# A GRU and mixture-of-experts kernel: the hidden bias of the candidate gate moves from VectorE's reset operation to a TensorE matmul

## The chip, the cores and the metric

The kernel runs on one core of one Trainium2 chip. The metric is the device time of one execution in microseconds; the time before is 849.63 us, the median of 3 runs (849.52 to 850.55). TensorE multiplies, and writes its results to PSUM; VectorE, ScalarE and GpSimd (POOL in the profile) do the elementwise work; SyncE (SP) and ScalarE issue the loads and stores.

## The reference, cut to what matters

The first half is a GRU over 4 sequences of 512 steps with a state of 512, the second a mixture of four experts on its output. Only the GRU's cell is touched:

```
def cell(h, x):
    gi = x @ W_ih + b_ih
    gh = h @ W_hh + b_hh
    i_r, i_z, i_n = jnp.split(gi, 3, axis=-1)
    h_r, h_z, h_n = jnp.split(gh, 3, axis=-1)
    r = sigmoid(i_r + h_r)
    z = sigmoid(i_z + h_z)
    n = tanh(i_n + r * h_n)
    return (1.0 - z) * n + z * h
```

The last third of `b_hh`, here called b_hn, is inside `h_n` and so is multiplied by r. It can't be folded into the input part, as the other two thirds are. After the GRU come the logits `h @ Wg + bg`, the top two of four experts for each token, a capacity of 512 tokens per expert, and per expert gelu(tok @ W1) @ W2, scaled and added into the output.

## The kernel before, in words

**The steps.** Each sequence is cut into 16 segments that run side by side, so that a step works on 64 columns (4 sequences by 16 segments, COLS). A segment has 32 steps; before them each segment runs 40 steps over the input ahead of it to find its starting state: 20 rough ones (ROUGH) that use only the high fp16 half of weights and state, and then 20 exact ones. So there are 72 steps: 20 rough ones and 52 exact ones. Numbers are split into a high and a low fp16 half, and an exact product is three products (high by high, high by low, low by high).

**A step on the engines.** The state has four blocks of 128 rows (j = 0 to 3). The gates of block j lie in PSUM bank j, 64 columns each for r, z and the candidate. TensorE first adds the input part of r and z into the bank by a matmul with a diagonal matrix (`inject`, line 452), which waits until the `reset` of block j of the step before is done (semaphore rn_done, line 450). The matmul that carries start=True clears the bank's marks, so the candidate's 64 columns are overwritten by the first matmul that comes to them. Then come the matmuls with the weights (`unit`, line 442, 64 columns each, three for a product of blocks): 12 for each block k of the state in a rough step, in the order k = 0 to 3; 144 in an exact step, in the order written out as ORDER (line 261). Each k waits for the new state's block k (high_ready, line 490).

When bank j is done, ScalarE takes the sigmoid of r and z (`sig`, line 758), VectorE does `reset` (line 1203: candidate part plus b_hn times r) and `candidate_in` (line 1208: plus the input part), ScalarE the tanh (line 763), VectorE `one_less_z` (line 1212) and `blend` (line 1219, the state's high half, which releases TensorE), and in exact steps `keep_state` (line 1224). GpSimd makes z times h (`carry`, line 931) and the low halves of blocks 0 and 1 (line 939), VectorE those of blocks 2 and 3. The order on VectorE is written out by hand (`exact` and `rough`, lines 1245 to 1252):

```
exact = ((reset, 0), (candidate_in, 0), (reset, 1), (candidate_in, 1), (reset, 2),
         (one_less_z, 0), (candidate_in, 2), (blend, 0), (keep_state, 0), (one_less_z, 1),
         (reset, 3), (blend, 1), (candidate_in, 3), (one_less_z, 2), (keep_state, 1), (blend, 2), ...
```

ORDER begins with the injects of banks 0 and 1, the unit of bank 1 with block 0 of the state, the inject of bank 2, the units of banks 0 and 2 with block 0, the inject of bank 3, and then a unit with block 1.

**The fills.** The products of the input with W_ih (`fill`, line 434, 512 columns) are made ahead: the first chunk in fp32 before the steps (lines 407 and 417), 24 matmuls just before the first step, and then 18 in each of the steps 0 to 21 and 12 in step 22. In rough steps they are spread over k by FILLS = (13, 2, 2, 1). Between its step work VectorE also splits these products and the recurrent weights (`other_work`).

**Before the steps.** VectorE takes the absolute maxima of all that is loaded (line 1062), from them the scales (lines 1090 to 1099 and 1139 to 1143), then splits W_ih (line 1118) and the first chunk of x (line 1124, `x_low`), whose semaphore x_split releases the first fill. ScalarE's queue issues two loads of W_ih and five small loads, of which that of bg (line 688) is the last.

Of the kernel before, what the change touches and what calls it, by code (L numbers as in the profile page):

```python
# [14 lines left out]
ALU = mybir.AluOpType  # L15
ACT = mybir.ActivationFunctionType
AX = mybir.AxisListType
RMAX = bass.bass_isa.ReduceOp.max
F32 = mybir.dt.float32
F16 = mybir.dt.float16  # L20
# [3 lines left out]
P = 128  # L24
# [9 lines left out]
SEARCH_PASSES = 10  # L34


def gru_moe(nc, x, x_t, cond_t, w_ih, w_hh, b_ih, b_hh, wg, bg, w1, w2, hs_rows, out):
    NB, T, D = x.shape
    N = NB * T
    E, _, H = w1.shape  # L40
# [15 lines left out]
    with ExitStack() as ctx:  # L56
        def sb(name, shape, dt=F32):
            return ctx.enter_context(nc.sbuf_tensor(name, shape, dt))
# [54 lines left out]
        def gru_tmp(n):  # L113
# [62 lines left out]
        un_y = sb("un_y", [P, 1])  # L176
        un_gates = sb("un_gates", [P, 1])
        gates_scale = sb("gates_scale", [P, 1])
        bhn_s = sb("bhn_s", [P, KD])
        neg_scale = sb("neg_scale", [P, 1])  # L180
        worst = sb("worst", [P, 4])
        flag = sb("flag", [P, SEG + 1], I32)
# [41 lines left out]
        names = """small_loaded out_init consts_pool consts_dve bias_ready  # L224
             gi_mm gi_high gi_low gi_kept diag_ready sig_done gates_known gi_known x_known wih_high wih_split whh_high x_high x_split peak_ready peak_known chain whh_ready zh_done warmed high_ready state_done low_ready last_low_ready gates_mm rn_done
            candin_ready tanh_done ocand_done start_saved check_a worst_ready worst_mm flag_ready
            gru_over turned wg_split lg_mm lg_kept sq_done probs_in probs_stored group_made rows_copied rows_stored steps_made exp_in exp_done
            above_ready chunk_peaks total_mm masks_ready sums_ready eq_mm sel_ready pos_mm pos_ready slots_ready list_mm idx_ready
            tok_turned tokT_ready ffn1_mm hid_ready ffn2_mm y_ready scattered latched w_peak w_peak_all w_scaled w_high w_low prep hid_made hid_high y_scaled tok_high
            tables again orders_made first_high first_low root rechain sp_waited pool_waited dve_waited pe_waited act_waited pool_consts""".split()  # L230
# [165 lines left out]
        def _(pe):  # L396
# [51 lines left out]
            def inject(j, c, cols, parts, steps):  # L448

                pe.wait_ge(S["rn_done"], steps + j + 1)  # L450
                for part in parts:
                    pe.matmul(gate_ps[:, j, 0:2, :], diag[:, :], gi_rz[:, c, j, part, :, cols],  # L452
                              start=(part == HIGH), stop=False, skip_group_check=True)

            def logits(i):

# [40 lines left out]

            fill(0, PREFILL)
            pe.wait_ge(S["diag_ready"], 1)
            pe.wait_ge(S["whh_high"], KD)  # L500
            pe.wait_ge(S["gi_kept"], 12)
            for i in range(ROUGH):
# [177 lines left out]
        def _(act):  # L680
# [7 lines left out]
            act.dma_start(bg_sb[:, :], bg.rearrange("(o e) -> o e", o=1).to_broadcast([P, E])).then_inc(S["small_loaded"], 16)  # L688

            act.wait_ge(S["consts_dve"], 1)  # L690
            act.activation(worst[:, 3:4], ones[:, 0:1], ACT.Sigmoid).then_inc(S["tables"], 1)
            act.wait_ge(S["tables"], 1)

# [327 lines left out]

        @block.vector
        def _(dve):
            dve.memset(ones[:, :], 1.0).then_inc(S["consts_dve"], 1)
            dve.memset(onesb[:, :], 1.0)
            dve.memset(flag[:, :], 0)
# [32 lines left out]
            def peak_of(dst, src, axes=AX.XY):  # L1059

                link_n[0] += 1
                dve.tensor_reduce(dst, src, axes, ALU.max, apply_absolute_value=True).then_inc(S["chain"], 1)

            for k in range(2):
                dve.wait_ge(S["first_loaded"][k], 32)
                peak_of(x_peak[:, k:k + 1], x_first[:, 2 * k:2 * k + 2, :])
                peak_of(chunk_peak[:, k:k + 1], wih_sb[:, 2 * k:2 * k + 2, 0:D])
            dve.wait_ge(S["wih_loaded"][1], 16)
            peak_of(chunk_peak[:, 2:3], wih_sb[:, :, D:2 * D])
            dve.wait_ge(S["small_loaded"], 16 * 5)  # L1070
# [38 lines left out]
            def rz_low(t):  # L1109

                c, m = TILES[t]
                dve.wait_ge(S["gi_high"], rz_count(t + 1))
                dve.tensor_tensor(gi_rz[:, c, m % 4, LOW, m // 4, :], gi_full[:, rz_count(t) % GI_RING, :],
                                  gi_rz[:, c, m % 4, HIGH, m // 4, :], ALU.subtract).then_inc(S["gi_low"], 1)
# [24 lines left out]
            dve.tensor_tensor(un_gates[:, :], unscale[:, WHH:WHH + 1], unscale[:, STATE:STATE + 1], ALU.mult)  # L1139
            link(dve.tensor_tensor(gates_scale[:, :], scale[:, WHH:WHH + 1], scale[:, STATE:STATE + 1], ALU.mult))  # L1140
            dve.tensor_scalar(neg_scale[:, :], scale[:, STATE:STATE + 1], -1.0, None, ALU.mult)
            dve.tensor_scalar(bhn_s[:, :], bhh[:, 8:12], gates_scale[:, 0:1], None, ALU.mult)
            link(dve.tensor_scalar(bsum_g[:, :], bsum[:, :], gates_scale[:, 0:1], None, ALU.mult))
            dve.sem_inc(S["gates_known"], 1)
            wih_low(0)
# [15 lines left out]
            for m in range(ACT_HIGHS, 8):  # L1161
                rz_high(m)
                rz_low(m)

            def whh_low(n):

# [22 lines left out]
            def step(gi_n, after, src, base, low, moved=False, ahead=(), between=()):  # L1189
# [10 lines left out]

                def reset(j):
                    dve.wait_ge(S["sig_done"], base + j + 1)
                    dve.scalar_tensor_tensor(rn[:, j, :], gate_ps[:, j, 2, :], bhn_s[:, j:j + 1], rz[:, j, 0, :],  # L1203
                                             ALU.add, ALU.mult).then_inc(S["rn_done"], 1)

                def candidate_in(j):
                    dve.wait_ge(S["rn_done"], base + (KD + j + 1))
# [446 lines left out]
def laid_out(inputs):  # L1654

    x = np.asarray(inputs['x'])
    nb, t, d = x.shape
    kd, steps = d // P, t // SEG

    x_t = x.reshape(nb * SEG, steps, kd, P).transpose(3, 2, 1, 0).reshape(P, kd, -1, 512).transpose(0, 2, 1, 3)  # L1660
    return {
        'x': x,
        'x_t': x_t,
        'cond_t': np.asarray(inputs['cond_2048']).reshape(nb, kd, P).transpose(2, 1, 0),
        'w_ih': inputs['L0_cond_W_ih'],
        'w_hh': inputs['L0_cond_W_hh'],
        'b_ih': np.asarray(inputs['L0_cond_b_ih']).reshape(-1, P).T,
        'b_hh': np.asarray(inputs['L0_cond_b_hh']).reshape(-1, P).T,
        'wg': np.asarray(inputs['L0_ffn_Wg']).reshape(kd, P, -1).transpose(1, 0, 2),
        'bg': inputs['L0_ffn_bg'],  # L1670
        'w1': inputs['L0_ffn_W1'],
        'w2': inputs['L0_ffn_W2'],
    }
# [19 lines left out]
```

## Time and profile before

| | |
|---|---|
| median of 3 runs | 849.63 us |
| the profiled execution | 849.56 us, of which the span from first to last instruction is 847.8 us |
| TensorE (PE) busy | 806.1 us, 95% of the span |
| VectorE (DVE) busy | 621.8 us, 73% |
| ScalarE (ACT) busy | 422.8 us, 50% |
| GpSimd (POOL) busy | 184.7 us, 22% |
| chain that ended last | PE 83%, DVE 11%, issue 2%, ACT 2%, DMA 1% |
| the steps | from 58.45 us to about 446 us of the span |

A matmul's busy time in the profile is its latency (193 ns for 64 columns), and many of them overlap; how closely they follow each other is read from the starts of the rows of a timeline, or from the chain of waits, whose pieces lie end to end.

### The profile page before, as it was taken

How to read it: one execution, taken by the hardware profiler on the slowest of the kernel's cores; microseconds unless marked ns; L12 is line 12 of the kernel's file. 1: busy time of each engine (PE TensorE's matmuls, PEld its weight loads, DVE VectorE, ACT ScalarE, POOL GpSimd, SP SyncE). 2: the span in 40 equal slices, each digit the busy share in tenths (PEclk: the TensorE clock that was granted, in tenths of full speed). 3: DMA queues.
4: the chain of work that ended last, by engine and by line, in shares of the span. 5: the costliest groups of instructions: out<-in, count | busy, mean ns of one | idle time of the engine just before them, and what ended most of it. 6: DMA issues, size and time to landing. Idle time of an engine off the chain costs nothing.

```text
span 847.8 us, 27827 instructions
## 1 busy us (share of the span) xinstructions
PE 806.1 (95%) x11579; PEld 520.9 (61%) x11580; DVE 621.8 (73%) x2104; ACT 422.8 (50%) x884; POOL 184.7 (22%) x459
## 2 busy tenths in 40 slices
PE   7999999999999999999995789999999999999996
PEld 3446656588989899999983444444444444544442
DVE  6969899868888888888886988685768566855400
ACT  0677676645566555555553437451745175417500
POOL 1002222223433333343330030121012101210011
PEclk9999999999999999999996999999999999999998
DMA  9900000000111010000002942454245424540011
GB/s 334 358 3 3 2 2 2 2 3 16 54 54 42 17 41 5 4 4 4 5 4 52 246 155 95 155 148 101 88 160 150 98 84 164 141 107 0 1 26 25
DMA packets 24280, 62.61 MB, mean 74 GB/s; under 512 B 4384, under 2 KB 4384, under 8 KB 22304
## 3 DMA queue, kind: packets, MB, share of 16 engines
q1 hardware_dynamic: 19312, 51.42, 18.0%
q0 software_dynamic: 3584, 8.42, 5.4%
q8 instruction: 86, 1.41, 0.7%
q10 hardware_dynamic: 1264, 1.08, 0.4%
q14 instruction: 34, 0.28, 0.1%
HBM read 52.49 MB, written 12.62 MB: 77 GB/s over the span
## 4 chain that ended last, share of the span: by engine, by line
PE 83%; DVE 11%; issue 2%; ACT 2%; DMA 1%; POOLq 0%; DVEq 0%
PE ps L442 22%; PE ps L649 20%; PE ps L662 20%; PE ps L434 10%; PE ps L417 3%; DVE wa L1203 3%; DVE wa L1208 2%; PE ps L452 2%; PE ps L407 2%; DVE halves L1219 2%; ACT wa L758 2%; PE ps L636 1%; DMA hx<-hs_rows,idx 1%; DVE ocand L1212 1%; PE ps L590 1%
## 5 line engine op out<-in xcount | busy, mean ns | idle before, releaser
L442 PE MATMUL ps<-halves,wa 128*128 128x64 f16 x8448 | 287.6, 193 | 5.6 <-DVE halves L1219 1.8
L442 PEld LDWEIGHTS ps<-halves,wa 128*128 128x128 f16 x8448 | 271.0, 98 | 33.1 <-DVE halves L1219 14.1
L662 PE MATMUL ps<-big 128*128 128x512 f16 x768 | 166.9, 379 | 0.0
L649 PE MATMUL ps<-hx,big 128*128 128x512 f16 x768 | 166.9, 379 | 0.0
L758 ACT ACTIVATE wa<-ps,un_gates 128x128 f32<-128x128 f32 x288 | 100.2, 366 | 106.6 <-PE ps L442 100.2
L662 PEld LDWEIGHTS ps<-big 128*128 128x128 f16 x768 | 75.2, 98 | 89.9
L649 PEld LDWEIGHTS ps<-hx,big 128*128 128x128 f16 x768 | 74.9, 98 | 89.9 <-issue 0.2
L763 ACT ACTIVATE wa<-wa,un_gates 128x64 f32<-128x64 f32 x288 | 99.1, 344 | 59.8 <-DVE wa L1208 53.3
L1203 DVE SCALAR_TENSOR_TENSOR wa<-ps,bhn_s,wa 128x64 f32<-128x64 f32 x288 | 80.0, 278 | 52.9 <-ACT wa L758 52.9
L434 PE MATMUL ps<-hx,wb 128*128 128x512 f16 x432 | 106.9, 379 | 1.0 <-issue 1.0
L840 ACT ACTIVATE hx<-ps,un_hid_in 128x512 f32<-128x512 f32 x64 | 43.7, 682 | 109.2 <-PE ps L649 109.2
L1219 DVE SCALAR_TENSOR_TENSOR halves<-ocand,neg_scale,wa 128x64 f16<-128x64 f32 (+1 forms) x288 | 86.2, 299 | 4.6 <-DVE ocand L1212 0.5
L1464 DVE SCALAR_TENSOR_TENSOR big<-wa,scale,big 128x2048 f16<-128x2048 f32 x28 | 65.3, 2349 | 25.0 <-ACT big L826 25.0
L1582 DVE SCALAR_TENSOR_TENSOR big<-hx,hid_scale,big 128x512 f16<-128x512 f32 x64 | 47.8, 749 | 36.2 <-ACT big L843 35.1
L826 ACT ACTIVATE big<-wa,scale 128x2048 f16<-128x2048 f32 x28 | 54.8, 1988 | 34.1 <-DVEq L1452 34.1
L1208 DVE TENSOR_TENSOR wa<-wa,big 128x64 f32<-128x64 f32 x288 | 65.8, 228 | 5.0
L452 PE MATMUL ps<-big,diag 128*128 128x128 f16 x496 | 62.1, 219 | 0.8 <-DVE wa L1203 0.4
L1212 DVE SCALAR_TENSOR_TENSOR ocand<-wa 128x64 f32<-128x64 f32 x288 | 62.4, 217 | 0.2
L1410 DVE TENSOR_REDUCE chunk_peak<-wa 128x1 f32<-128x2048 f32 x28 | 62.0, 2277 | 0.0
L434 PEld LDWEIGHTS ps<-hx,wb 128*128 128x128 f16 x432 | 37.9, 98 | 35.7 <-issue 1.8
L931 POOL TENSOR_TENSOR wa<-wa,hx 128x64 f32<-128x64 f32 x128 | 42.6, 333 | 78.9 <-ACT wa L758 74.3
L997 POOL DMA_INDIRECT out<-hx,idx_out x16 | 29.0, 1815 | 136.1 <-DVE hx L1588 136.1
(209 smaller groups left out, 711.8 us busy)
## 6 DMA issues: line engine op xcount, KB each, us to landing
wa<-in_w SPq DMA_DIRECT2D x28, 1024.0 KB, 5.3
hs_rows<-big SPq DMA_DIRECT2D x8, 512.0 KB, 5.6
big<-in_w_hh SPq DMA_DIRECT2D x4, 768.0 KB, 19.4
wb<-in_w SPq DMA_DIRECT2D x12, 256.0 KB, 2.6
big<-in_w_ih SPq DMA_DIRECT2D x2, 1024.0 KB, 12.4
hx<-in_x_t SPq DMA_DIRECT2D x2, 1024.0 KB, 16.4
big<-in_w_ih ACTq DMA_DIRECT2D x2, 512.0 KB, 6.7
wa<-in_x_t SPq DMA_DIRECT2D x2, 512.0 KB, 6.3
```

Of the source, the lines that this page charges most:

```text
L434: mm = pe.matmul(ps[:, gi_bank(tile), :], wih_parts[:, w, k, m * P:(m + 1) * P], x_parts[:, q, t, k, :], start=(left == 0), stop=(left == ...
L442: mm = pe.matmul(gate_ps[:, j, g, :], whh_parts[:, k, w, (4 * g + j) * P:(4 * g + j + 1) * P], halves[:, src, k, h, :], start=False, stop= ...
L452: pe.matmul(gate_ps[:, j, 0:2, :], diag[:, :], gi_rz[:, c, j, part, :, cols], start=(part == HIGH), stop=False, skip_group_check=True)
L649: mm = pe.matmul(ps[:, m % 2, :], w1p[:, w, k, m * P:(m + 1) * P], tokT[:, t, k, :], start=(k == 0 and n == 0), stop=(k == KD - 1 and n == 2))
L662: mm = pe.matmul(ps[:, 2 + g % 2, :], hid[:, h, k, g * P:(g + 1) * P], w2p[:, w, k, :], start=(k == 0 and n == 0), stop=(k == KH - 1 and n ...
L758: act.activation(rz[:, j, :, :], gate_ps[:, j, 0:2, :], ACT.Sigmoid, scale=un_gates[:, 0:1]).then_inc(S["sig_done"], 1)
L763: act.activation(cand[:, j, :], cand_in[:, j, :], ACT.Tanh, scale=un_gates[:, 0:1]).then_inc(S["tanh_done"], 1)
L1203: dve.scalar_tensor_tensor(rn[:, j, :], gate_ps[:, j, 2, :], bhn_s[:, j:j + 1], rz[:, j, 0, :], ALU.add, ALU.mult).then_inc(S["rn_done"], 1)
L1208: dve.tensor_tensor(cand_in[:, j, :], rn[:, j, :], gi_n(j), ALU.add).then_inc(S["candin_ready"], 1)
L1212: dve.scalar_tensor_tensor(ocand[:, j, :], rz[:, j, 1, :], -1.0, cand[:, j, :], ALU.add, ALU.mult).then_inc(S["ocand_done"], 1)
L1219: dve.scalar_tensor_tensor(high_of(j), old(ocand_, j), neg_scale[:, 0:1], old(zh_, j), ALU.mult, ALU.add).then_inc(S["high_ready"], 1)
L1464: dve.scalar_tensor_tensor(w_parts[which][:, LOW, cols], stage[:, cols], scale[:, which:which + 1], w_parts[which][:, HIGH, cols], ALU.mul ...
```

## The change

b_hn is added by one more matmul in `inject`, with a stationary operand of 64 partitions. It is zero but for partition 0, which holds b_hn rounded to fp16 (scaled), and partition 32, which holds what the rounding left over. The moving operand is a 64 by 64 block of one value. `reset` becomes a product of two tensors. The row is loaded twice by ScalarE's queue, and VectorE makes the two halves in the part before the steps.

```diff
@@ inject
                 for part in parts:
                     pe.matmul(gate_ps[:, j, 0:2, :], diag[:, :], gi_rz[:, c, j, part, :, cols],
                               start=(part == HIGH), stop=False, skip_group_check=True)
+                pe.matmul(gate_ps[:, j, 2, :], bhn_parts[:, j * P:(j + 1) * P], bhn_unit[:, :], start=False, stop=False,
+                          skip_group_check=True)
@@ TensorE, before the first step
             pe.wait_ge(S["diag_ready"], 1)
+            pe.wait_ge(S["bhn_split"], 1)
@@ ScalarE, after its seven loads
             act.wait_ge(S["consts_dve"], 1)
+            for row in ROW_OF:
+                act.dma_start(bhn_row[row:row + 1, :], b_hn).then_inc(S["bhn_loaded"], 16)
             act.activation(worst[:, 3:4], ones[:, 0:1], ACT.Sigmoid).then_inc(S["tables"], 1)
@@ VectorE, its first instruction
+            dve.memset(bhn_row, 0.0)
             dve.memset(ones[:, :], 1.0).then_inc(S["consts_dve"], 1)
@@ VectorE, after the maxima of the first halves of x and of W_ih's first third
+            dve.wait_ge(S["bhn_loaded"], 32)
+            b_peak, b_scale, b_un = (bhn_scales[:, i:i + 1] for i in range(3))
+            link(dve.tensor_reduce(b_peak, bhn_row, AX.X, ALU.max, apply_absolute_value=True))
+            link(dve.tensor_scalar(b_peak, b_peak, 1e-30, None, ALU.max))
+            link(dve.tensor_scalar(b_un.bitcast(I32), b_peak.bitcast(I32), 0x7F800000, None, ALU.bitwise_and))
+            dve.tensor_scalar(b_scale.bitcast(I32), b_un.bitcast(I32), -1.0, float((254 + SCALE_TO) << 23),
+                              ALU.mult, ALU.add)
+            link(dve.tensor_scalar(b_un.bitcast(I32), b_un.bitcast(I32), -float(SCALE_TO << 23), None, ALU.add))
+            link(dve.tensor_scalar(bhn_parts[:, :], bhn_row, b_scale, None, ALU.mult))
+            lows_row = slice(ROW_OF[1], ROW_OF[1] + 1)
+            dve.scalar_tensor_tensor(bhn_parts[lows_row, :], bhn_row[lows_row, :], b_scale[lows_row, :],
+                                     bhn_parts[lows_row, :], ALU.mult, ALU.subtract)
             dve.wait_ge(S["wih_loaded"][1], 16)
             peak_of(chunk_peak[:, 2:3], wih_sb[:, :, D:2 * D])
@@ VectorE, at the scales of the gates
-            dve.tensor_scalar(bhn_s[:, :], bhh[:, 8:12], gates_scale[:, 0:1], None, ALU.mult)
@@ VectorE, before the first step
+            dve.tensor_scalar(bhn_unit[:, :], ones[0:COLS, 0:COLS], b_un, gates_scale[0:COLS, 0:1], ALU.mult,
+                              ALU.mult).then_inc(S["bhn_split"], 1)
@@ reset
-                    dve.scalar_tensor_tensor(rn[:, j, :], gate_ps[:, j, 2, :], bhn_s[:, j:j + 1], rz[:, j, 0, :],
-                                             ALU.add, ALU.mult).then_inc(S["rn_done"], 1)
+                    dve.tensor_tensor(rn[:, j, :], gate_ps[:, j, 2, :], rz[:, j, 0, :], ALU.mult).then_inc(S["rn_done"], 1)
```

`ROW_OF` is (0, 32); `bhn_row` is the first 64 partitions of the tile `carried` (512 fp32 values each), which the steps use later; `bhn_parts` is 64 by 512 in fp16, `bhn_unit` 64 by 64 in bf16. `link` makes VectorE wait for the instruction it has just issued.

## Rows read from the trace of the kernel before

**Rows 1.** Groups of instructions by line and shape: count, busy us, mean ns of one, idle before
```profile
L442 PE MATMUL ps<-halves,wa 128*128 128x64 f16 x8448 | 287.6, 193 | 5.6 <-DVE halves L1219 1.8
...
L1203 DVE SCALAR_TENSOR_TENSOR wa<-ps,bhn_s,wa 128x64 f32<-128x64 f32 x288 | 80.0, 278 | 52.9 <-ACT wa L758 52.9
...
L1208 DVE TENSOR_TENSOR wa<-wa,big 128x64 f32<-128x64 f32 x288 | 65.8, 228 | 5.0
...
L1224 DVE SCALAR_TENSOR_TENSOR hx<-ocand,neg_scale,wa 128x64 f32<-128x64 f32 x128 | 36.6, 286 | 0.0
```

**Rows 2.** Chain of waits, a rough step: start us, length us, what
```profile
133.44 2.81 PE ps L434 x13
...
136.30 0.09 PE ps L442 x3
...
138.95 2.81 PE ps L434 x13
```

**Rows 3.** Timeline, an exact step: start us, length of the merged group us, engine, line
```profile
344.48 1.16 ACT L758 ACTIVATE wa<-ps,un_gates 128x128 f32<-128x128 f32 x3 [1.61 <-PE ps L442]
...
345.53 0.73 ACT L763 ACTIVATE wa<-wa,un_gates 128x64 f32<-128x64 f32 x2
...
345.99 0.21 DVE L1212 SCALAR_TENSOR_TENSOR ocand<-wa 128x64 f32<-128x64 f32 x1
...
346.22 0.38 PE L452 MATMUL ps<-big,diag 128*128 128x128 f16 x4
346.31 0.28 DVE L1219 SCALAR_TENSOR_TENSOR halves<-ocand,neg_scale,wa 128x64 f16<-128x64 f32 x1
...
346.65 0.35 PE L442 MATMUL ps<-halves,wa 128*128 128x64 f16 x6
...
347.04 0.41 DVE L1219 SCALAR_TENSOR_TENSOR halves<-ocand,neg_scale,wa 128x64 f16<-128x64 f32 x1
347.06 0.30 POOL L939 TENSOR_TENSOR halves<-hx,halves 128x64 f16<-128x64 f32 x1
...
347.29 0.28 PE L452 MATMUL ps<-big,diag 128*128 128x128 f16 x2
...
347.50 0.46 PE L442 MATMUL ps<-halves,wa 128*128 128x64 f16 x10
...
349.57 0.37 ACT L758 ACTIVATE wa<-ps,un_gates 128x128 f32<-128x128 f32 x1 [1.60 <-PE ps L442]
```

**Rows 4.** Timeline of TensorE at rough step 11
```profile
121.82 2.97 PE L434 MATMUL ps<-hx,wb 128*128 128x512 f16 x13
125.02 0.23 PE L452 MATMUL ps<-big,diag 128*128 128x128 f16 x1 [0.23 <-DVE halves L1219]
```

**Rows 5.** Timeline of VectorE before the steps, with its idle time and what ended it
```profile
11.60 3.40 DVE L1062 TENSOR_REDUCE chunk_peak<-big 128x1 f32<-128x1024 f32 x2
15.50 0.17 DVE L1071 TENSOR_TENSOR bsum<-bih,bhh 128x8 f32<-128x8 f32 x1 [0.49 <-DMA bg_sb<-in_bg]
...
21.32 4.54 DVE L1062 TENSOR_REDUCE x_peak<-hx 128x1 f32<-128x2048 f32 x3 [0.21 <-DMA hx<-in_x_t]
...
48.96 1.41 DVE L1124 SCALAR_TENSOR_TENSOR hx<-hx,scale 128x512 f16<-128x512 f32 x2
```

**Rows 6.** Timeline of TensorE at the first fill
```profile
50.47 1.89 PE L434 MATMUL ps<-hx,wb 128*128 128x512 f16 x8 [1.02 <-issue]
```

**Rows 7.** Timeline of ScalarE's queue: the last of its small loads is issued
```profile
4.26 0.49 ACTq L688 DMA_DIRECT2D bg_sb<-in_bg  x1
```

**Rows 8.** DMA issues by line: count, KB each, median us from issue to landing
```profile
bhh<-in_b_hh ACTq DMA_DIRECT2D x1, 6.0 KB, 8.9
...
bg_sb<-in_bg ACTq DMA_DIRECT2D x1, 2.0 KB, 11.2
```

**Rows 9.** Stretches: length us, busy time per engine, granted clock share (PEclk), DMA share, GB/s
```profile
455.70:460.63 4.93, 4.91 (x35) 4.29 (x36) 2.85 (x14) 2.35 (x4) 0.00 (x0) 0.50 0.01 2
...
494.76:498.18 3.42, 3.42 (x11) 1.86 (x10) 1.38 (x2) 0.97 (x2) 0.81 (x1) 0.50 0.41 131
```

More of the change, by code:

```diff
@@ L34, with gru_moe @@
 SEARCH_PASSES = 10
-def gru_moe(nc, x, x_t, cond_t, w_ih, w_hh, b_ih, b_hh, wg, bg, w1, w2, hs_rows, out):
+def gru_moe(nc, x, x_t, cond_t, w_ih, w_hh, b_ih, b_hh, b_hn, wg, bg, w1, w2, hs_rows, out):
     NB, T, D = x.shape
@@ L178, in gru_moe @@
         gates_scale = sb("gates_scale", [P, 1])
-        bhn_s = sb("bhn_s", [P, KD])
+        bhn_row = carried[0:COLS, :, :, :].rearrange("p d k c -> p (d k c)")
+        bhn_parts = sb("bhn_parts", [COLS, D], F16)
+        bhn_unit = sb("bhn_unit", [COLS, COLS], BF16)
+        bhn_scales = sb("bhn_scales", [COLS, 4])
+        ROW_OF = (0, 32)
         neg_scale = sb("neg_scale", [P, 1])
@@ L226, in gru_moe @@
             candin_ready tanh_done ocand_done start_saved check_a worst_ready worst_mm flag_ready
-            gru_over turned wg_split lg_mm lg_kept sq_done probs_in probs_stored group_made rows_copied rows_stored steps_made exp_in exp_done
+            gru_over turned bhn_loaded bhn_split wg_split lg_mm lg_kept sq_done probs_in probs_stored group_made rows_copied rows_stored steps_made exp_in exp_done
             above_ready chunk_peaks total_mm masks_ready sums_ready eq_mm sel_ready pos_mm pos_ready slots_ready list_mm idx_ready
@@ L1668, in laid_out @@
         'b_hh': np.asarray(inputs['L0_cond_b_hh']).reshape(-1, P).T,
+        'b_hn': np.asarray(inputs['L0_cond_b_hh'])[2 * d:].reshape(1, -1),
         'wg': np.asarray(inputs['L0_ffn_Wg']).reshape(kd, P, -1).transpose(1, 0, 2),
```

## The prediction

> **What bounds the kernel now.** I read the chain of waits first, since TensorE's 95% is an average over parts with different limits. The chain shows two kinds of steps, and before them a part that ends on VectorE.
>
> Rough steps with fills belong to TensorE. In [rows 2] the pieces lie end to end and the step repeats after 138.95 - 133.44 = 5.51 us, with VectorE nowhere in it. Two paces come from here: 0.09 / 3 = 0.029 us for a matmul of 64 columns, 2.81 / 13 = 0.216 for one of 512. Steps 20 to 22 carry their fills at the head and are alike up to bank 0 of step 22, so 23 steps belong to TensorE.
>
> Exact steps without fills repeat after 349.57 - 344.48 = 5.09 us [rows 3], and here the timeline says more than the chain. The four injects start at 346.22 and, by 0.38 less their latency of about 0.22 over three gaps, follow each other by 0.055, so TensorE could go on at 346.44. It goes on at 346.65, 0.05 after blend 0 ended (346.31 + 0.28). Then it comes to block 1: the last injects start at 347.29 and 347.35, it could go on at 347.40, and it goes on at 347.50, 0.05 after blend 1 ended (347.04 + 0.41). So TensorE stands 0.21 and 0.10 us per step. From 347.50 it runs through 63 matmuls to the end of bank 0 and the next sigmoid. The loop is: sigmoid 0, three resets and candidates on VectorE, one_less_z 0, blend 0, blend 1, TensorE. It holds steps 22 to 70, 49 periods.
>
> Before the steps TensorE stands 1.02 us ahead of its first fill [rows 6]. The profile gives no releaser, but the last x_low ends at 48.96 + 1.41 = 50.37 and the fill starts at 50.47 [rows 5, 6]: VectorE's preparation ends last. It waits only briefly for loads after 11.60 (0.49, 0.21, and two alike of 0.30 and 0.21), and from 21.32 it works nearly without a gap [rows 5].
>
> **The change, part by part.** *The added matmuls.* Four per step, 288 in all. No matmul with 64 partitions is in the trace. The nearest row is the 64-column one [rows 1]: its pace of 0.029 us is my value. It could be as low as nothing where TensorE stands anyway, and as high as 0.33, if the array had to empty before and after it (latency 0.193 less 0.029, twice). In the 23 steps that belong to TensorE, nothing hides them: 23 x 4 x 0.029 = +2.7 us. In step 11 TensorE stands for VectorE: the fills from 121.82 end at 121.82 + 13 x 0.216 = 124.63 and the inject starts at 125.02 [rows 4], 0.39 us. Later arrival of TensorE and shorter resets close this: -0.4. Sum for these steps: +2.3.
>
> *The reset.* It becomes a product of two tensors. The other kind of instruction with a per-partition operand and both inputs in SBUF takes 286 ns, reset with an input in PSUM 278, the tensor product or sum without such an operand 228 [rows 1]. So the 50 to 60 ns hang on that operand and not on PSUM; I take 0.22, and a saving of 0.055 in length and in the distance to the next instruction. Its bounds are 0 and 0.065. In an exact step three resets lie ahead of blend 0, which would be 0.165. But one_less_z 0 needs tanh 0, and that one starts at 345.53 behind sigmoid 2 on ScalarE and ends at about 345.87, whatever VectorE does [rows 3]. one_less_z can start at 345.90 instead of 345.99: the saving is capped at 0.09. All behind it moves by 0.09, blend 1 included, which ends at 347.36, and TensorE may go on at 347.41.
>
> *The added matmuls in an exact step.* Two come before blend 0 and fit into the 0.21 that TensorE stands (0.12 left with the earlier blend). Two lie between blend 0 and the units of block 1: from 346.56, 18 x 0.029 + 4 x 0.055 + 2 x 0.029 = 0.81, so 347.37, still ahead of 347.41. They are hidden, by 0.04. If a reset saved nothing, they would still fit into the 0.10. So an exact step gains 0.09, and 49 of them -4.4 us (bounds 0 and, see below, -6.6).
>
> *VectorE before the steps.* The new block waits for two loads and stands ahead of the maxima of W_ih's second third, at 12.73, ahead of the second reduction in the group at 11.60 (whose end, 15.00, less the 2.27 of 2048 elements, is where it starts) [rows 5]. The loads are issued behind bg's, which is issued at 4.26 for 0.49 [rows 7], so at about 4.8 and 5.3. bg lands at 4.26 + 11.2 = 15.5, small ones need 8.9 or more [rows 8]: between 14.2 and 17, I take 16.0. Then come a maximum over 512 elements (2.27 for 2048 gives 1.1 ns each; 0.7 with its start and its link), three linked small ones at 0.2, one at 0.1, a scaling of 512 elements, 0.5, and a subtraction on one partition but 512 long, 0.7: 2.6 us. So the second third begins at 18.6 instead of 12.73. VectorE had 1.2 us of waits for loads behind this point, and these and no more take it up, with the bias sum now behind its load: it is at the scales 4.3 us later. From there to the last x_low nothing is idle that could give it back, and TensorE's first fill starts 4.3 us later. Queued behind VectorE's wait are the scales (ScalarE waits on them for its whole part before the steps) and x_low, for which TensorE waits. With the load at 14.2 it is 2.5, with 17 it is 5.3, and if the load were there when VectorE comes, 1.1. The memset of 512 elements at the start, about 0.5 us at that rate, lies beside VectorE's wait for the first loads; without that cover it would cost itself. The product for bhn_unit, 0.2 us, lies beside the 24 fills.
>
> *The clock.* TensorE then stands 5 us instead of 1. In two places of the trace TensorE comes back to dense work after it stood for some us, and both times it works at a granted clock of 0.50 first: through the 4.93 us before 460.63, and 3.42 us from 494.76 [rows 9]. At half clock half of such a stretch is lost: 1.7 us, bounds 0 and 2.5.
>
> **The sum.** +4.3 + 1.7 + 2.3 - 4.4 = +3.9. The profiled execution took 849.56, 847.8 of it the span and 1.8 around it; the median of the runs, 849.63, is the same within 0.1. So 847.8 + 3.9 + 1.8 = 853.5 us.
>
> **The rivals.** *The array empties at each added matmul.* It uses half the rows, between matmuls that use all. For it: nothing in the trace mixes the two. Against: nothing either. The price from the latency is 0.33 per added matmul. Rough and fill steps: 23 x 4 x 0.33 = 30. In an exact step the path from blend 0 gets 2 x 0.33 and the pair before it some 0.6 beyond its cover, so about 1.1 in place of a gain of 0.09: 55. With the part before the steps: near 940 us. The Trainium skill, "TensorEngine Tiling (Array Packing)", section "Key Properties", says that changing the tiling mode, not just the tile, drains TensorE, and lists a contraction of 64 or less as the case for row tiling; the trace of before can't show it. By that rule the sum would be the one of this rival, without it the one above. I give it 0.14.
>
> *The load is early (the other side).* If the row is in SBUF when VectorE comes to it, the block costs 2.6 less the waits behind it, 1.1, TensorE stands 2 us, and the clock stays: 1.1 + 2.3 - 4.4 = -1.0, so 848.6. It decides from a landing before about 14, where the time falls below that of before. For it: it is 2 KB to one partition, and bg's load, 128 rows, was the slowest of the five. Against: it is issued behind bg on the same queue, while the large loads run. 0.15.
>
> *The reset is no shorter from PSUM.* Then the exact steps gain nothing: 847.8 + 8.3 + 1.8 = 857.9. Against: PSUM is no dearer in reset's own row. 0.09.
>
> *Blend 1 loses its stretch.* It takes 0.41 where blend 0 takes 0.28, and GpSimd's low half starts 0.02 behind it [rows 3]. Moved ahead by 0.09 it may end before the two meet. Then TensorE's own path, 347.37, is last, and a step gains 0.135: -6.6 in place of -4.4, 851.3. 0.12.
>
> **How the numbers follow.** The forecast has 0.50. Its own range is 850.9 to 856.5, from the bounds of landing, clock and the cap. The range over the cases is 847.5 to 862: it holds the early load, the missing saving and a dearer matmul of up to 0.1 in rough steps, and leaves the emptying array out. Under 0.2% (1.7 us) this kernel's measurement can't tell from no change. Faster needs the early load together with the blend's gain or a still smaller block: 0.11. The same: most of the rest of the early load, and the low end of the blend case, 0.14. Slower 0.75.
>
> **What would show it.** Right: an added matmul 0.03 us behind the inject before it; rough steps of 5.63 us; reset at 0.22 us; exact steps of 5.00 us with TensorE standing less than 0.1 before blend 0's units; VectorE's wait for the row ending near 16 and the first fill near 54.8; a granted clock of half for about 3.4 us behind it. Wrong: exact steps of 5.09 or more, a first fill before 53, rough steps above 5.7 us, which would be the emptying array, or an idle time of VectorE ahead of the resets that takes the gain back.

## The result, and the profile after

The changed kernel takes 900.99 us (median of 4 runs, 899.23 to 901.1) beside 849.75 for the kernel before on the same chip: a ratio of 1.0596, with an interval of 1.0578 to 1.0615. The forecast was 853.5 us with a range of 847.5 to 862, so it is wrong, and by far. What happened is close to what the prediction named as its first rival: the added matmul costs TensorE far more than its 64 columns. The profiled execution has a span of 897.5 us, 49.7 more than before. It is the shortest of the four (899.23); the other three took 900.91 to 901.10, at a mean granted clock of 0.982 to 0.983 beside its 0.985.

The page's head and its busy times:

```profile
span 897.5 us, 28413 instructions
...
PE 859.3 (96%) x11867; PEld 547.7 (61%) x11868; DVE 616.6 (69%) x2112; ACT 421.0 (47%) x884; POOL 183.9 (20%) x459
```

The groups by line and shape (count, busy us, mean ns of one, idle before) that answer to [rows 1]:

```profile
L446 PE MATMUL ps<-halves,wa 128*128 128x64 f16 x8448 | 297.1, 193 | 0.9 <-DVE halves L1242 0.8
...
L1231 DVE TENSOR_TENSOR wa<-wa,big 128x64 f32<-128x64 f32 x288 | 71.7, 249 | 5.0
...
L1227 DVE TENSOR_TENSOR wa<-ps,wa 128x64 f32<-128x64 f32 x288 | 63.0, 219 | 107.6 <-ACT wa L767 107.6
...
L458 PE MATMUL ps<-bhn_unit,bhn_parts 64*128 64x64 bf16 x288 | 57.5, 200 | 0.0
```

The added matmul (L458) has a mean of 200 ns, only 7 more than a unit (L446). That mean hides its cost: a matmul's length here is mostly latency, and several are under way at once. What it costs is in the distances between starts. The reset (L1227) did become shorter, 219 ns for 278, yet VectorE's wait ahead of it doubled, from 52.9 us to 107.6: the gain was in an engine that now waits longer.

A rough step in the chain of waits (start us, length us, what; in the chain a piece lasts only until the next one takes over), as in [rows 2]:

```profile
142.99 2.81 PE ps L438 x13
145.80 0.06 PE ps L456
145.85 0.13 PE ps L458
145.99 0.19 PE ps L446 x3
```

Before, the inject (L452 there) took 0.06, in the same chain as [rows 2]:

```profile
136.25 0.06 PE ps L452
```

With the three units behind it that was 0.06 + 0.09 = 0.15 us. Now inject, added matmul and units take 0.06 + 0.13 + 0.19 = 0.38. The chain puts only 0.13 on the added matmul; the rest, 0.10, is on the three units behind it, which took 0.09 before. So a reader of the chain alone would find only half of the cost under the new line.

TensorE in an exact step (start us, length of the merged group us), answering to [rows 3]:

```profile
351.38 0.27 PE L456 MATMUL ps<-big,diag 128*128 128x128 f16 x2
351.59 0.20 PE L458 MATMUL ps<-bhn_unit,bhn_parts 64*128 64x64 bf16 x1
351.72 0.28 PE L456 MATMUL ps<-big,diag 128*128 128x128 f16 x2
351.94 0.20 PE L458 MATMUL ps<-bhn_unit,bhn_parts 64*128 64x64 bf16 x1
352.07 0.35 PE L446 MATMUL ps<-halves,wa 128*128 128x64 f16 x6
```

The second inject of the pair at 351.38 starts at about 351.43, and the added matmul only at 351.59; the next inject starts 0.13 behind it. Medians over all steps of the distance from start to start: inject to added 152 ns, added to unit 132, added to inject 132, where before inject to inject is 56 and unit to unit 29. So each added matmul costs about 0.10 us ahead of it, 0.10 behind it, and 0.03 of its own: 0.152 + 0.132 - 0.056 = 0.228 us. The state is ready all this time. TensorE no longer stops for VectorE at 352.07, where it stopped in [rows 3]: its own path is longer than VectorE's.

Where the 49.7 us are, from the start of the first inject of each step:

| part | before | after | difference |
|---|---|---|---|
| before the first step | 58.45 | 61.63 | +3.2 |
| steps 0 to 21 (the rough ones, and two exact ones with fills) | 127.72 | 147.99 | +20.3 |
| steps 22 to 39 (exact, no logits) | 92.97 | 101.55 | +8.6 |
| step 40 | 5.74 | 6.01 | +0.3 |
| steps 41 to 70 (exact, with logits) | 153.26 | 171.0 | +17.7 |
| the rest | | | -0.3 |

A price of 0.229 per added matmul (the distances give 0.228) comes near every line; a rough step alone grew by a little more, from 5.51 to 6.46, which is 0.24 for each. Steps 0 to 21: 22 x 4 x 0.229 = 20.2. An exact step gets 4 x 0.229 = 0.92, less what TensorE stood before. That was the 0.21 and 0.10 of [rows 3] with the four small logits matmuls, which leaves 0.61 (measured 5.70 for 5.09). In steps without logits it stood their 0.10 more, which leaves 0.51 (measured 5.60). Times 18 and 30 that is 9.2 and 18.3; the table has 0.6 less in each, since some steps of before took more than 5.09 (5.27 to 5.88) and had more time to hide it in.

VectorE before the steps, answering to [rows 5], and the first fill, to [rows 6]:

```profile
15.04 0.68 DVE L1080 TENSOR_REDUCE bhn_scales<-carried 64x1 f32<-64x512 f32 x1 [2.38 <-DMA carried<-in_b_hn]
...
16.87 0.74 DVE L1088 SCALAR_TENSOR_TENSOR bhn_parts<-carried,bhn_scales,bhn_parts 1x512 f16<-1x512 f32 x1
17.62 2.29 DVE L1072 TENSOR_REDUCE chunk_peak<-big 128x1 f32<-128x2048 f32 x1
```

```profile
53.65 8.15 PE L438 MATMUL ps<-hx,wb 128*128 128x512 f16 x37 [3.83 <-issue]
```

VectorE waits 2.38 us for the row, the block takes 17.62 - 15.04 = 2.58, and the first fill starts 3.18 later than in [rows 6]. In this execution TensorE stood 3.83 us and came back at full clock (the row gives the length, busy time and instructions of each engine, and then the granted share, 1.00):

```profile
53.65:61.60 7.95, 7.95 (x37) 3.62 (x38) 4.09 (x9) 5.56 (x9) 0.00 (x0) 1.00 0.00 1
```

### The profile page after: what moved, and what is told of

It reads as the page before. It is cut to its first block, busy times and chain, and to the rows that moved or that the text cites. A ratio compares the mean times of both kernels' runs of the same rounds, so it can differ in the third digit from the quotient of the medians.

```text
span 897.5 us, 28413 instructions
## 1 busy us (share of the span) xinstructions
PE 859.3 (96%) x11867; PEld 547.7 (61%) x11868; DVE 616.6 (69%) x2112; ACT 421.0 (47%) x884; POOL 183.9 (20%) x459
## 4 chain that ended last, share of the span: by engine, by line
PE 87%; DVE 7%; DMA 2%; issue 2%; ACTq 1%; ACT 0%; POOLq 0%; POOL 0%; DVEq 0%
PE ps L446 29%; PE ps L656 18%; PE ps L669 18%; PE ps L438 10%; PE ps L458 4%; PE ps L456 4%; DMA carried<-in_b_hn 1%; PE ps L643 1%; DMA hx<-hs_rows,idx 1%; DVE chunk_peak L1152 1%; DVE x_peak L1072 1%; PE ps L597 1%; DVE wb L1140 1%; PE ps L586 1%; DVE chunk_peak L1072 0%
## 5 line engine op out<-in xcount | busy, mean ns | idle before, releaser
L446 PE MATMUL ps<-halves,wa 128*128 128x64 f16 x8448 | 297.1, 193 | 0.9 <-DVE halves L1242 0.8
L446 PEld LDWEIGHTS ps<-halves,wa 128*128 128x128 f16 x8448 | 266.8, 98 | 22.3 <-DVE halves L1242 1.2
L1227 DVE TENSOR_TENSOR wa<-ps,wa 128x64 f32<-128x64 f32 x288 | 63.0, 219 | 107.6 <-ACT wa L767 107.6
L1242 DVE SCALAR_TENSOR_TENSOR halves<-ocand,neg_scale,wa 128x64 f16<-128x64 f32 (+1 forms) x288 | 80.7, 280 | 4.8 <-issue 0.5
L456 PE MATMUL ps<-big,diag 128*128 128x128 f16 x496 | 75.3, 220 | 0.0
L1231 DVE TENSOR_TENSOR wa<-wa,big 128x64 f32<-128x64 f32 x288 | 71.7, 249 | 5.0
L458 PE MATMUL ps<-bhn_unit,bhn_parts 64*128 64x64 bf16 x288 | 57.5, 200 | 0.0
```

The costliest lines, as they stand in the source:

```text
L446: mm = pe.matmul(gate_ps[:, j, g, :], whh_parts[:, k, w, (4 * g + j) * P:(4 * g + j + 1) * P], halves[:, src, k, h, :], start=False, stop= ...
L458: pe.matmul(gate_ps[:, j, 2, :], bhn_parts[:, j * P:(j + 1) * P], bhn_unit[:, :], start=False, stop=False, skip_group_check=True)
L1227: dve.tensor_tensor(rn[:, j, :], gate_ps[:, j, 2, :], rz[:, j, 0, :], ALU.mult).then_inc(S["rn_done"], 1)
L1231: dve.tensor_tensor(cand_in[:, j, :], rn[:, j, :], gi_n(j), ALU.add).then_inc(S["candin_ready"], 1)
L1242: dve.scalar_tensor_tensor(high_of(j), old(ocand_, j), neg_scale[:, 0:1], old(zh_, j), ALU.mult, ALU.add).then_inc(S["high_ready"], 1)
```

## The experiments

Two theories at the start. The first: the price belongs to the change between a matmul over 64 rows of the array and its neighbours over 128, paid once on the way in and once on the way out. The second: it belongs to something else that is new, the write into the third 64 columns between other writes, the mixed bf16 and fp16 operands, or the extra load of weights. Four kernels change only that matmul (and, for 128 and 96 partitions, make its operands on all partitions); the kernel before beside them has a median of 849.34 (847.96 to 850.25, 13 runs). Four more take the other steps of the prediction apart, beside a median of 849.65 (846.86 to 851.77, 20 runs).

### The same matmul over 128 partitions

The edit, in short:

```diff
-bhn_row = carried[0:COLS, :, :, :]
+bhn_row = carried[:, :, :, :]
-bhn_parts = sb("bhn_parts", [COLS, D], F16); bhn_unit = sb("bhn_unit", [COLS, COLS], BF16)
+bhn_parts = sb("bhn_parts", [P, D], F16);    bhn_unit = sb("bhn_unit", [P, COLS], BF16)
```

The added rows are zero, so the sum stays what it was.

> The changed kernel with the added matmul over 128 partitions, the other rows zero (row, halves and unit on 128 partitions). In the changed kernel a matmul comes 0.152 us behind the inject before it instead of 0.055, and the next one 0.132 behind it instead of 0.029: 0.20 us for a matmul on part of the array. Theory A (the array changes its tiling mode and empties, twice per added matmul): the price is gone, 0.055 and 0.029; rough steps 5.63 us, exact steps 5.00, first fill still at 53.7; in all 849.7 + 3.2 + 2.3 - 4.4 = 850.8 us. Theory B (the price hangs on the operands, bf16 beside fp16, or on writing the same PSUM bank as the injects): 0.152 and 0.132 stay, near 901 us.

Measured: 851.41 us (848.12 to 851.76, 10 runs), a ratio of 1.0014 [1.0002, 1.0025]. One exact step on TensorE:

```profile
345.20 0.27 PE L456 MATMUL ps<-big,diag 128*128 128x128 f16 x2
345.31 0.19 PE L458 MATMUL ps<-bhn_unit,bhn_parts 128*128 128x64 bf16 x1
345.34 0.28 PE L456 MATMUL ps<-big,diag 128*128 128x128 f16 x2
345.45 0.19 PE L458 MATMUL ps<-bhn_unit,bhn_parts 128*128 128x64 bf16 x1
345.56 0.35 PE L446 MATMUL ps<-halves,wa 128*128 128x64 f16 x6
```

Inject to added is 0.056, added to inject 0.03. With the same operands' types, place and weight loads, the 0.20 are gone: the second theory falls.

The load of the weights (PEld) shows where the time goes. These are the first loads for the added matmul in the two steps shown, in the changed kernel and in this one:

```profile
351.58 0.09 PEld L458 LDWEIGHTS ps<-bhn_unit,bhn_parts 64*128 64x128 f16 x1
```

```profile
345.26 0.10 PEld L458 LDWEIGHTS ps<-bhn_unit,bhn_parts 128*128 128x128 f16 x1
```

With 128 partitions the load starts 0.002 us behind the start of the inject in front, 0.054 ahead of its own matmul (medians over all 288). With 64 it starts only 0.147 behind the inject, 0.004 ahead of its matmul. So at the change TensorE no longer loads the next weights right behind the start of the matmul in front.

The rough step in the chain, as in [rows 2]:

```profile
142.55 0.06 PE ps L456
142.60 0.03 PE ps L458
142.63 0.09 PE ps L446 x3
```

A rough step takes 5.62 us and an exact one 4.99 to 5.00; the prediction had 5.63 and 5.00 with a matmul at 0.029. ScalarE's sigmoids show the exact period, answering to those of [rows 3]:

```profile
348.45 1.15 ACT L767 ACTIVATE wa<-ps,un_gates 128x128 f32<-128x128 f32 x3 [1.60 <-PE ps L446]
...
353.44 0.81 ACT L767 ACTIVATE wa<-ps,un_gates 128x128 f32<-128x128 f32 x2 [1.60 <-PE ps L446]
```

### Where the price begins: 96 and 32 partitions

The edits to the changed kernel's line, in short; the first kernel also makes its operands on 128 partitions:

```diff
-pe.matmul(gate_ps[:, j, 2, :], bhn_parts[:, j * P:(j + 1) * P], bhn_unit[:, :], ...)
+pe.matmul(gate_ps[:, j, 2, :], bhn_parts[0:96, j * P:(j + 1) * P], bhn_unit[0:96, :], ...)   # the first
+pe.matmul(gate_ps[:, j, 2, :], bhn_parts[0:32, j * P:(j + 1) * P], bhn_unit[0:32, :], ...)   # the second
```

> As k128, but the matmul reads 96 of the partitions. Theory A1 (only a mode of 64 or 32 rows needs the change, 96 rows run in the mode of the full array): 0.055 and 0.029 us, near 851 us. Theory A2 (any matmul that leaves rows idle pays): 0.152 and 0.132, near 901 us.

> The changed kernel with the added matmul over 32 partitions, so without the row on partition 32: the low half of b_hn is left out. Theory A1 (a change of mode costs what it costs): 0.152 and 0.132 us as with 64 rows, near 901 us. Theory C (the price follows the number of rows that are switched off): above 0.152 and 0.132, over 910 us.

Measured, one run each: 851.6 us with 96 partitions, 899.68 with 32. TensorE at the injects, first with 96, then with 32:

```profile
346.56 0.27 PE L456 MATMUL ps<-big,diag 128*128 128x128 f16 x2
346.67 0.19 PE L458 MATMUL ps<-bhn_unit,bhn_parts 96*128 96x64 bf16 x1
346.70 0.28 PE L456 MATMUL ps<-big,diag 128*128 128x128 f16 x2
```

```profile
346.75 0.27 PE L456 MATMUL ps<-big,diag 128*128 128x128 f16 x2
346.96 0.20 PE L458 MATMUL ps<-bhn_unit,bhn_parts 32*128 32x64 bf16 x1
347.09 0.29 PE L456 MATMUL ps<-big,diag 128*128 128x128 f16 x2
```

With 96 the distances are 55 and 34 ns, with 32 they are 152 and 131, the same as with 64. So it isn't that rows are left out: 96 leaves 32 out and pays 5 ns (a rough step takes 5.64 us for 5.62). The price has two levels and no slope, as a change of the array's configuration would have it. Where between 64 and 96 it begins wasn't tried.

### Paid per change, not per matmul

The edit, in short and in the order of the operations:

```diff
 # rough step, k == 0
-for j in range(KD):
-    inject(j); bhn(j); units(0, j)
+for j in range(KD): inject(j)
+add_bhn(0, 1, 2, 3)
+for j in range(KD): units(0, j)
 # exact step: banks 0 and 1 together behind inject 1, banks 2 and 3 as they were
```

> The changed kernel with its 64-row matmuls next to each other where the order allows: in rough steps all four behind the four injects, in exact steps those of banks 0 and 1 together. Theory A (the price belongs to the change, 0.097 in and 0.103 out, and not to the matmul): neighbours follow each other at 0.03 us; rough steps 6.46 - 3 x 0.20 = 5.86 us, exact steps 5.70 - 0.20 = 5.50; 901 - 12 - 10 = 879 us. If each such matmul pays by itself (a weight load that isn't hidden): 6.46 and 5.70 stay, 901 us.

Measured: 878.36 us (877.65 and 879.07), a ratio of 1.0341 [1.0321, 1.0362]. The chain in a rough step:

```profile
140.57 0.22 PE ps L456 x4
140.80 0.22 PE ps L461 x4
141.02 0.46 PE ps L446 x12
```

Four added matmuls have 0.22 here, and the twelve units 0.46, where 12 x 0.029 would be 0.35: 0.10 ahead of the group, 0.10 behind it, and 0.03 to 0.04 for each member. The distance from added to added is 38 ns for the first two of a group and 29 from then on, which is the pace of the units. A rough step takes 5.83 for 6.46 (0.63 less; three changes in and out saved at 0.20 are 0.60). An exact step has three groups in place of four and takes 5.39 and 5.49, by 0.21 less. The 64-row matmuls next to each other pay at most 0.01 among themselves. This is the direct evidence that the price is for going from matmuls of one kind to the other and back, and not for each matmul. The kernel was expected at 879.

The Trainium skill, "TensorEngine Tiling (Array Packing)", section "Key Properties", says that changing the tiling mode drains TensorE. These traces agree that each change costs time, and add the price, 0.20 us for the way there and back. The page lists row tilings of 64 and 32 rows, and none of 96; that fits the two levels. Whether the array really empties isn't shown: the latency less the pace would be 0.164 each way, measured is 0.10, and the weight load that comes late takes 0.09 to 0.10 itself. Emptying and a load that is no longer made ahead weren't taken apart.

### VectorE's half of the change alone

```diff
 # in the kernel before
-dve.scalar_tensor_tensor(rn[:, j, :], gate_ps[:, j, 2, :], bhn_s[:, j:j + 1], rz[:, j, 0, :], ALU.add, ALU.mult)
+dve.tensor_tensor(rn[:, j, :], gate_ps[:, j, 2, :], rz[:, j, 0, :], ALU.mult)
```

> The kernel before with reset as the plain product and nothing in place of b_hn, which is left out of the computation: the reset's gain alone. If the gain is capped by tanh 0 behind sigmoid 2 on ScalarE, exact steps take 5.00 us, no less, though three resets ahead of blend 0 are 0.055 shorter each (0.165 would give 4.93); rough steps stay at 5.51; 849.5 - 4.4 - 0.4 = 844.7 us.

This kernel leaves b_hn out, so it isn't a version of the kernel that could be used; it shows what the reset's form is worth. Measured: 843.17 us (841.47 to 844.24, 4 runs), a ratio of 0.9936 [0.9914, 0.9958]. An exact step:

```profile
349.99 1.15 ACT L758 ACTIVATE wa<-ps,un_gates 128x128 f32<-128x128 f32 x3 [1.60 <-PE ps L442]
...
351.04 0.65 ACT L763 ACTIVATE wa<-wa,un_gates 128x64 f32<-128x64 f32 x2
...
351.41 0.23 DVE L1211 SCALAR_TENSOR_TENSOR ocand<-wa 128x64 f32<-128x64 f32 x1
```

From sigmoid 0 to one_less_z 0 (L1211) it is 351.41 - 349.99 = 1.42, where [rows 3] have 345.99 - 344.48 = 1.51. One_less_z follows the end of tanh 0 (351.04 + 0.34 = 351.38) by 0.03, as the cap in the prediction says. The next sigmoid 0 starts at 354.97, a period of 4.98. The 49 exact periods gain their 0.1 each. The time is 1.5 us below the expected 844.7: in the profiled execution, the shortest of the four, the steps up to 70 gave 5.7 us, and another 0.65 came before the first step and 1.8 from the start of the last one on, where the edit changes next to nothing.

### TensorE's half alone

The edit, in short:

```diff
 # 128-row matmul, its preparation behind the last x_low, TensorE waits for it only before the first inject
-dve.tensor_tensor(rn[:, j, :], gate_ps[:, j, 2, :], rz[:, j, 0, :], ALU.mult)
+dve.scalar_tensor_tensor(rn[:, j, :], gate_ps[:, j, 2, :], bhn_s[:, j:j + 1], rz[:, j, 0, :], ALU.add, ALU.mult)
```

with a bhn_s of zeros, so that VectorE's reset has its old form and length (278 ns).

> The added matmul over 128 partitions, b_hn's halves made late (after the splits before the first step, with TensorE's wait moved to just before the first inject), but reset kept as the operation with a per-partition operand, which is now zero: the added matmuls' price alone. If they are hidden in exact steps by the time that TensorE stands: 5.09 us there and 5.63 in rough steps, 849.5 + 2.7 = 852 us. If they are not hidden: 5.15 to 5.21 in exact steps, 855 to 858 us.

Measured: 851.28 us (850.46 to 852.37, 8 runs), a ratio of 1.0023 [1.0009, 1.0038]. Two sigmoid groups:

```profile
347.42 1.16 ACT L771 ACTIVATE wa<-ps,un_gates 128x128 f32<-128x128 f32 x3 [1.60 <-PE ps L447]
...
352.51 0.81 ACT L771 ACTIVATE wa<-ps,un_gates 128x128 f32<-128x128 f32 x2 [1.60 <-PE ps L447]
```

The exact step takes 5.09, as before, although TensorE has four matmuls more: they are hidden, as the prediction worked out. Rough steps take 5.62, 0.11 more, which is four at 0.029.

### The preparation moved, and the matmul only where it is hidden

The edit of the 128-row kernel, in short:

```diff
-            dve.wait_ge(S["bhn_loaded"], 32)       # ... with the block behind it, at 11.6 us
             ...
+            dve.wait_ge(S["bhn_loaded"], 32)       # ... the same block, ahead of bhn_unit, behind the splits
-            pe.wait_ge(S["bhn_split"], 1)          # behind the 24 fills, before the first step
+            pe.wait_ge(S["bhn_split"], 1)          # just before the first inject
```

The second kernel adds to this:

```diff
-                pe.matmul(gate_ps[:, j, 2, :], bhn_parts[...], bhn_unit[...], ...)
+                if LOW in parts:                   # exact steps only
+                    pe.matmul(gate_ps[:, j, 2, :], bhn_parts[...], bhn_unit[...], ...)
 # reset: the plain product in exact steps, the old form with bhn_s in the 20 rough ones
```

> As k128, with the preparation of b_hn's halves moved behind the splits before the first step and TensorE's wait moved behind the 13 fills of step 0. If the preparation's price is its place in VectorE's chain before the first fill: first fill at 50.5 us, the granted clock stays at full, rough 5.63, exact 5.00: 849.5 + 2.3 - 4.4 = 847.4 us. If VectorE is late for step 0 instead: up to 2.6 more.

> As k128_late, but the matmul and the plain product only in the 52 exact steps; the 20 rough ones keep the reset of before, where VectorE has time and TensorE has none. Rough 5.51 us, exact 5.00: 849.5 + 0.4 (three steps with fills) - 4.4 = 845.5 us, faster than both kernels.

Measured: 845.86 us (844.87 to 846.79, 7 runs), 0.9961 [0.9946, 0.9976], for the first, and 844.94 (844.19 to 845.51, 6 runs), 0.9951 [0.9934, 0.9968], for the second. Sigmoids of the second:

```profile
346.82 1.15 ACT L772 ACTIVATE wa<-ps,un_gates 128x128 f32<-128x128 f32 x3 [1.61 <-PE ps L447]
...
351.80 0.37 ACT L772 ACTIVATE wa<-ps,un_gates 128x128 f32<-128x128 f32 x1 [1.60 <-PE ps L447]
```

Its rough steps are those of before (5.51), its exact ones take 4.98. The first inject starts at 58.36, for 58.45 before: with the block behind the splits nothing of it is on the path. This kernel computes the whole of the reference and is quicker than both the kernel before, by 4.7 us of medians (0.5%), and the changed one, by 56. That it is quicker than the first of the two isn't shown, since their intervals overlap: in the profiles it is 1.7 us shorter in steps 0 to 21 and 1.4 longer from the start of the last step on. The first was expected at 847.4 and came out 1.5 lower; in its profile 1.2 us of that are again in this last part. So the idea of the change holds; its 64 partitions and the place of its preparation don't.

The gain from the preparation's place is seen between the two 128-row kernels: first inject at 63.12 with the early block and at 58.41 with the late one, 4.7 us. The fills of the early one:

```profile
53.77 9.51 PE L438 MATMUL ps<-hx,wb 128*128 128x512 f16 x37 [4.59 <-issue]
```

```profile
53.16:56.57 3.41, 2.80 (x7) 1.02 (x8) 3.08 (x7) 3.11 (x6) 0.00 (x0) 0.50 0.00 0
```

and of the late one:

```profile
50.43 8.14 PE L438 MATMUL ps<-hx,wb 128*128 128x512 f16 x37 [0.35 <-issue]
```

53.77 - 50.43 = 3.34 us is the later start of the fills, and 9.51 - 8.14 = 1.4 is the half clock of the stretch from 53.16 to 56.57.

## Why the prediction was wrong

**The step that failed** is the first term of the change, the added matmul: "The nearest row is the 64-column one [rows 1]: its pace of 0.029 us is my value." It measured 0.229. Neither did the time that TensorE stands hide it in the exact steps: four of them are 0.92 us where TensorE stood 0.31, so a step took 5.70 for 5.09 and not 5.00. Rough steps took 6.46, which the prediction had listed as the sign of the emptying array (above 5.7). The text saw that the trace has no matmul over 64 partitions and named the cost of 0.33 as the upper bound, but then took the row that was like it in columns. In what counts, the rows of the array that it uses, no row was near, and a chance of 0.14 for the rival was too little. The rival was right that a lone 64-row matmul pays on the way in and on the way out, and its size was too large: 0.33 came from the latency less the pace, twice; measured is 0.10 each way, and 0.229 with the matmul's own pace. Its parts were 30, 55 and 6 us and led to 940; measured are 20.3 in the steps 0 to 21, 26.6 in the exact ones and 3.2 before them, 50.1 in all.

**The range** reached to 862, "a dearer matmul of up to 0.1 in rough steps", and left the rival out. It was drawn on the side of the likeliest case although the rival lay 86 us above the forecast.

**What held.**
- The reset: 219 ns for 278, and the cap by tanh 0 behind sigmoid 2. The plain product alone gives a step of 4.98 to 4.99, not the 4.93 of a saving of 0.165. The end of blend 0 came 0.075 to 0.08 us nearer to sigmoid 0 (0.09 forecast).
- The cover of the added matmuls in exact steps, if they are over 128 rows: they cost no period, as TensorE's half alone (5.09) and the 128-row kernel (4.99) show. The words "They are hidden, by 0.04" don't fit the 128-row kernel, though: see rival 4.
- Rough steps at 5.63: 5.62 with 128 rows. Step 11, where a stand of 0.39 was to close, went from 5.91 to 5.75 there, with 0.12 added: only 0.28 of the 0.39 came back.
- The block on VectorE, 2.6 us: 2.58. The row landed at 15.0 for 16.0, so the path got 3.2 for 4.3. Its steps with the landing (2.5 for 14.2, 4.3 for 16.0) give 3.3 for 15.0, so the landing was put 1.0 too late. One term in it was off: with 1.2 us of waits taken up, 18.6 - 12.73 - 1.2 would be 4.7 and not 4.3. Measured, W_ih's second third began 4.9 later (17.62 for 12.73) and the first of the scales 3.3 (30.05 for 26.73), so 1.6 was taken up.

**What was open.** The clock term, +1.7, came out as nothing in the profiled execution of the changed kernel (it stood 3.83 us and went on at full clock) and as 1.4 in the 128-row one. It can't be told which it is from how long TensorE stands: see below. The other three executions took 1.7 to 1.9 us more at a lower mean clock, which is what such a stretch would cost, but where in them the clock fell isn't known.

**Rival 4**, a blend 1 that loses its stretch, happened: with 128 rows it took 0.28 for 0.41, and TensorE's own path came last at block 1, as the rival says. TensorE went on with block 1's units 0.03 behind the matmul in front and 0.154 behind the end of blend 1, where before it followed that end by 0.058 (medians over steps 26 to 39 and 44 to 68). The next VectorE instruction lies beside GpSimd's low half instead and is stretched in its place:

```profile
345.93 0.28 DVE L1242 SCALAR_TENSOR_TENSOR halves<-ocand,neg_scale,wa 128x64 f16<-128x64 f32 x1
...
346.02 0.36 POOL L948 TENSOR_TENSOR halves<-hx,halves 128x64 f16<-128x64 f32 x1
...
346.13 0.33 DVE L1231 TENSOR_TENSOR wa<-wa,big 128x64 f32<-128x64 f32 x1
```

But the step gained no 0.135, it gained 0.10, and the traces show why: the prediction's loop lacks a wait. TensorE doesn't run freely from block 1 to the end of bank 0. Its 61st matmul from there needs the state's last low half (block 3), which VectorE makes, here the second of this pair:

```profile
347.69 0.41 DVE L1266 TENSOR_TENSOR halves<-hx,halves 128x64 f16<-128x64 f32 x2
```

That matmul starts 0.057 behind the end of this low half in the kernel before, in the 128-row kernels and with the plain product alone, and the next sigmoid 0 follows 0.30 later. From sigmoid 0 to the end of the low half it is 4.735 us before and 4.636 with 128 rows (medians over steps 44 to 68): that is the whole of the 0.10. The distance to the matmul in front is 0.036 us before, 0.059 with 128 rows and 0.117 without the added matmuls. So with 128 rows TensorE has only 0.03 left there, and without the added matmuls it would only wait longer.

**With measured terms** the sum closes, for the 128-row kernel with early preparation: span 847.8 + 3.3 (later fills) + 1.4 (clock) + 2.3 (rough steps) - 4.9 (49 exact steps at 0.10) + 1.8 around the span = 851.7, measured 851.41. Only the 2.3 and the 1.8 are the forecast's own.

## What to carry to other kernels

Before a matmul of another shape is put between others, ask which of its dimensions is new to the array, and bound by that one; in this kernel a matmul over 64 or 32 rows among matmuls over 128 cost 0.20 us beyond its columns wherever it stood alone. So pad its operands with zero rows to 128, or put such matmuls next to each other. Read the cost of a matmul in the distances between starts, since its mean length (200 ns for 193) shows none of it, and the chain puts half on the next line. Before you count on a gain in a loop, look for every wait in it, also for those that are nearly covered: here the wait for the last low half, which held TensorE by less than 0.01 us before, set what the step gained. A preparation that is needed late belongs behind the one that is needed first, even if it is small.

## What the runs showed of the hardware

- A matmul over 64 or 32 partitions between ones over 128 starts 0.10 us later than its neighbour's pace allows, and the next one again 0.10 later; over 96 partitions it pays 0.005; those over 64 next to each other follow by 0.029 to 0.038. The weights for it are loaded 0.004 us ahead of it, where with 128 or 96 partitions it is 0.054.
- The clock after a stand. TensorE stood 3.83 us in the changed kernel and came back at a granted clock of 1.00. With 32 partitions it stood 3.70 and had 0.50 from 54.56 to 57.98; with 96 it stood 3.69, and with the grouped matmuls 3.19, and had 0.50 for 6.83 us. With 128 partitions it stood 4.59 and had 0.50 for 3.41. The same order of work ahead of it gave 0, 1.4, 1.7, 2.5 or 2.9 us of loss by the fills' lengths (8.15, 9.51, 9.83, 10.69, 11.01, with 64, 128, 32 and 96 partitions and grouped). The 128-row kernel's runs spread by 3.6 us (848.12 to 851.76), but so do those of the kernel before, which stands only 1.02 us there (846.86 to 851.77 in one session), so that the spread comes from this place isn't shown. The stretch with 96 partitions:

```profile
51.95:58.78 6.83, 5.19 (x13) 1.88 (x14) 5.74 (x12) 5.93 (x8) 0.00 (x0) 0.50 0.00 0
```

- The reset with a per-partition operand and the added sum takes some 56 ns more than the plain product, at 128x64 (277 for 221, both in the one kernel that has both forms of the reset):

```profile
L1234 DVE TENSOR_TENSOR wa<-ps,wa 128x64 f32<-128x64 f32 x208 | 45.9, 221 | 43.4 <-ACT wa L772 43.4
...
L1237 DVE SCALAR_TENSOR_TENSOR wa<-ps,bhn_s,wa 128x64 f32<-128x64 f32 x80 | 22.2, 277 | 6.8 <-ACT wa L772 6.7
```
